# Attention's rows, their low halves and a router step in another order on VectorE, in a fused attention and expert kernel

## The chip, the cores and the metric

One core of a Trainium2 chip. The metric is the device time of one launch in microseconds; the time of a kernel is the median of its runs. The core has five engines that run their own instruction queues in order: TensorE (PE: matrix products; weight loads stand as PEld), VectorE (DVE), ScalarE (ACT), GpSimd (POOL) and SyncE (SP), which here only issues transfers. They wait for one another on semaphores.

## The reference

A pre-norm block of a sequence model, in float32, with x of 4 sequences of 2048 tokens of 256 numbers:

```python
x = x + attn(layernorm(x))     # causal linear attention, 16 heads of 16
#   q = elu(x Wq + bq) + 1, k = elu(x Wk + bk) + 1, v = x Wv + bv
#   s += k v^T ; z += k ; row = (q s) / (q z + 1e-6) ; out = rows Wo + bo
x = x + moe(layernorm(x))      # 8 experts 256 -> 512 (gelu) -> 256
#   each token goes to its top 2 experts by logits, weighted by a softmax of the two
```

## The kernel before

The program has two parts. The first, on which the change bears, is a chain of iterations over the sequence; the second runs the experts on tiles of 256 token rows and is untouched.

Attention works in steps of 128 tokens of each of the 4 sequences (`b` = 0 to 3), 16 steps in all. Each tile that feeds a product is split into a high half and a low half in float16 (value minus high), so that products of float16 tiles keep nearly float32 accuracy: ScalarE writes the high half, VectorE (for q and k: GpSimd) the low one. The names end in `_hi`/`_high` and `_lo`/`low`.

The iterations are pipelined over four stages, and the function `body(j, c)` of each engine writes its part of iteration `c` by hand, in the order in which the engine's queue will run it:

- `fr`, the front of step c: norm 1 of x, transposes (`x_transposes`), projections of q and k (`project(0)` to `project(3)`, `feature`, `qk_high`), values of v, and the transfers that stack the parts of q and k.
- `bk`, attention of step c - 1: for each b four groups of scores, `scores(b, n)` on TensorE, `score_hi(b, n)` on ScalarE, `score_lo(b, n)` on VectorE; then `attend(b)` (48 small products with the values, and the update of the state), `attention(b)` on VectorE (division by the denominator, L1293 to L1300, tile `at`), `state_part(b)` (L1309), the transpose of the rows (`out_transpose`, L693, into pA), their halves (`out_hi` L1031, `out_lo` L1314, tile `aT`), `out_project(b)`, and `residual(b)`, which adds x, writes `x1` (L1340) and takes the statistics of norm 2. Row 3 of a step is finished in the next iteration.
- `ro`, the router of step c - 2: norm 2 (`norm2_shift` L1287, `norm2_apply` L1039), and `router()` on VectorE: logits (L1367, L1369), top 2 of 8 (L1373, L1377), counts (L1386).
- `sc`, step c - 3: TensorE sums the counts (`route_positions`), VectorE makes the slots (`router_slots`), GpSimd scatters the rows to the experts' lists in memory.

Iterations 0 and 1 fill the pipeline; 2 to 15 have a front, 16 to 18 drain it. `STEPS` is 16. During the iterations the weights of the experts are loaded and split as well (`w1_high` on ScalarE, `w1_low` L1415 on VectorE), and `norm1_stats`, `norm1_shift` (L1254) prepare x of the next step.

All of TensorE's projection results go through a few banks of PSUM. Bank pA is shared by the transposed rows, the router's logits and the output projection, so the transposes of row b wait for the logits of the row before (`lga_done`), and `out_project(b)` waits until `residual` of the row before has read the bank (`x1_done`).

In VectorE's order around the change, of which iteration 6 is looked at below, the pieces stand so: xT's low halves (L1274), score_lo(0, 0), out_lo(3), residual(2), score_lo(0, 1), row data, score_lo(0, 2), residual(3), score_lo(0, 3), slots, score_lo(1, 0), norm2_shift, attention(0), state_part(0), score_lo(1, 1), statistics of x, out_lo(0), score_lo(1, 2), and so on, and at the end out_lo(2), router, attention(3), state_part(3), the logits of row 2.

Of the kernel before, what the change touches and what calls it, by code (L numbers as in the profile page):

```python
# [104 lines left out]
def build(nc, x, wqkvo, bqk, bv, bo, rw, w1, b1, w2, b2, cf, ch, cb, cm, out):  # L105
# [5 lines left out]
    with ExitStack() as ctx:  # L111
# [443 lines left out]
        def _(pe):  # L555
# [9 lines left out]
            def body(j, c, front=True, back=True):  # L565
# [120 lines left out]
                def out_transpose(s, b):  # L686
                    g = 4 * s + b
                    pe.wait_ge(at_done, g + 1)
                    if g:

                        pe.wait_ge(lga_done, g)
                    for k in range(KC):
                        mm = nc.tensor.transpose(pA[:, k * C:(k + 1) * C], at[:, k * P:(k + 1) * P], ident)  # L693
                    mm.then_inc(aT_ps, 1)
# [234 lines left out]
        def _(act):  # L929
# [27 lines left out]
            def body(j, c, front=True, back=True):  # L957
# [143 lines left out]
                if fr:  # L1101
                    feature_exp(2)
                    qk_high(1)
                normed = ro and c != STEPS + 1
                if bk:
                    out_hi(s, 0)
                    score_hi(1, 2)
                    score_hi(1, 3)
                if fr:
                    feature(3)  # L1110
                    qk_high(2)
                if normed:
                    norm2_apply(0)
                if bk:
                    score_hi(2, 0)
# [8 lines left out]
                if normed:  # L1124
                    norm2_apply(1)
                if bk:
                    out_hi(s, 1)
                    score_hi(2, 2)
                if normed:
                    norm2_apply(2)  # L1130
# [92 lines left out]
        def _(dve):  # L1223
# [33 lines left out]
            def body(j, c, front=True, back=True):  # L1257
# [102 lines left out]
                def router():  # L1360
# [3 lines left out]
                    if c >= 4:  # L1364
# [5 lines left out]
                                                   ALU.mult, ALU.mult))  # L1370
                    carry_wait(dve)
# [120 lines left out]
                if sc and c not in (STEPS, STEPS + 1):  # L1492
                    router_slots()
                if bk:
# [10 lines left out]
                elif ro and c != STEPS + 1:  # L1505
                    norm2_shift()
# [7 lines left out]
                if bk:  # L1514
                    score_lo(1, 1)
                if ahead:
                    norm1_stats(i + 1, 0, 2)
                if c == STEPS + 1:
                    router()
                    for b in range(B):  # L1520
                        norm2_apply(b)
                if bk:
                    out_lo(s, 0)
# [11 lines left out]
                if bk:  # L1535
                    score_lo(2, 0)
                    residual(s, 0)
                    attention(1)
# [3 lines left out]
                    score_lo(2, 2)  # L1542
                if ahead:
# [3 lines left out]
                if bk:  # L1547
                    score_lo(2, 3)
# [16 lines left out]
                if ro and c != STEPS + 1:  # L1565
                    router()
                if bk:
                    attention(3)
                    state_part(3)
                    logit_part(s, 2)  # L1570
                if c == 1 and not front:
# [377 lines left out]
```

## Time and profile before

| | |
|---|---|
| median of 3 runs | 1016.1 us (1013.57 to 1018.55) |
| profiled execution, its time / its span | 1024.98 us / 1023.2 us |
| TensorE, weight loads busy | 913.0 us (89%), 740.2 us (72%) |
| VectorE, ScalarE, GpSimd busy | 758.2 us (74%), 680.7 us (67%), 658.2 us (64%) |
| iterations | to about 580 us, experts from about 603 us |
| granted TensorE clock, mean | 0.974 of full |

The span runs from the first to the last instruction of the profiled execution; the rest of its time lies around it. A busy share says how much of the span an engine had an instruction running. An engine that waits in its queue holds all that stands behind it, so the timelines are read for the idle time in front of an instruction, which stands in brackets with the engine and line that ended it.

### The profile page before, as it was taken

How to read it: one execution, taken by the hardware profiler on the slowest of the kernel's cores; microseconds unless marked ns; L12 is line 12 of the kernel's file. 1: busy time of each engine (PE TensorE's matmuls, PEld its weight loads, DVE VectorE, ACT ScalarE, POOL GpSimd, SP SyncE). 2: the span in 40 equal slices, each digit the busy share in tenths (PEclk: the TensorE clock that was granted, in tenths of full speed). 3: DMA queues.
4: the chain of work that ended last, by engine and by line, in shares of the span. 5: the costliest groups of instructions: out<-in, count | busy, mean ns of one | idle time of the engine just before them, and what ended most of it. 6: DMA issues, size and time to landing. Idle time of an engine off the chain costs nothing. (4 is left out here: it accounts for less than half of the span.)

```text
span 1023.2 us, 33647 instructions
## 1 busy us (share of the span) xinstructions
PE 913.0 (89%) x10722; PEld 740.2 (72%) x10723; DVE 758.2 (74%) x2280; ACT 680.7 (67%) x1295; POOL 658.2 (64%) x580
## 2 busy tenths in 40 slices
PE   6788899899989998999987559899999999999994
PEld 3577677767766677766766338678999999999994
DVE  5788788888898888889887566456666666666673
ACT  7868888898888888898875414445555555555552
POOL 3245877788778877887773543347655665656565
PEclk9999899999999999999998779999999999999998
DMA  6726744554455354645451743435655556555554
GB/s 172 203 76 204 249 126 147 170 161 136 150 152 176 124 152 149 182 128 147 139 156 44 283 136 69 69 60 94 95 95 90 98 89 98 89 98 88 94 92 50
DMA packets 102583, 131.31 MB, mean 128 GB/s; under 512 B 15056, under 2 KB 89296, under 8 KB 101648
## 3 DMA queue, kind: packets, MB, share of 16 engines
q1 hardware_dynamic: 74336, 92.54, 32.4%
q0 software_dynamic: 25680, 35.01, 18.6%
q10 hardware_dynamic: 2464, 2.38, 0.7%
q8 instruction: 64, 1.05, 0.5%
q14 instruction: 39, 0.32, 0.1%
HBM read 64.29 MB, written 65.60 MB: 127 GB/s over the span
## 5 line engine op out<-in xcount | busy, mean ns | idle before, releaser
L1907 POOL DMA_INDIRECT out<-yt,to_token x135 | 216.6, 1604 | 176.2 <-DMA out<-yt,to_token 80.4
L1269 DVE SCALAR_TENSOR_TENSOR ahl<-pS,ahl 128x512 f16<-128x512 f32 x240 | 161.2, 682 | 42.1 <-ACT ahl L980 39.7
L980 ACT ACTIVATE ahl<-pS 128x512 f16<-128x512 f32 x240 | 142.2, 599 | 49.8 <-PE pS L652 36.0
L1783 POOL DMA_INDIRECT expert_in<-xn,cur x128 | 131.1, 1024 | 30.8 <-issue 26.0
L1191 ACT ACTIVATE g<-pS,b1s 128x256 f32<-128x256 f32 (+1 forms) x140 | 57.3, 462 | 94.1 <-PE pS L562 94.1
L562 PE MATMUL pS<-gT,w1s 128*128 128x256 f16 (+1 forms) x840 | 96.8, 271 | 4.0 <-DVE gT L1697 4.0
L562 PE MATMUL pF<-w2s,ghl 128*128 x816 | 95.3, 273 | 2.4 <-issue 1.6
L1704 DVE TENSOR_TENSOR ghl<-g,ghl 128x1024 f16<-128x1024 f32 (+1 forms) x68 | 83.0, 1221 | 18.8 <-ACT ghl L1216 12.5
L1777 POOL TENSOR_TENSOR state<-state,ut 128x272 f32<-128x272 f32 x64 | 49.9, 779 | 72.2 <-DVE ut L1309 71.3
L562 PE MATMUL pU<-w2s,ghl 128*128 x804 | 94.4, 273 | 1.6 <-issue 1.1
L562 PE MATMUL pF<-xT,was 128*128 128x512 f16 x384 | 92.8, 379 | 3.2 <-DVE xT L1274 3.0
L673 PE MATMUL pO<-vhl,ahl 128*128 128x17 f16 x3072 | 90.4, 171 | 5.6 <-DVE ahl L1269 3.6
L673 PEld LDWEIGHTS pO<-vhl,ahl 128*128 128x128 f16 x3072 | 88.4, 96 | 8.5 <-DVE ahl L1269 4.4
L652 PE MATMUL pS<-qst,kst 128*128 128x256 f16 x480 | 92.9, 276 | 0.0
L562 PEld LDWEIGHTS pS<-gT,w1s 128*128 x840 | 80.6, 99 | 15.5 <-issue 5.2
L648 PE MATMUL pS<-cbs 128*128 128x384 bf16 x240 | 79.7, 332 | 12.7 <-DVE ahl L1269 9.1
L562 PEld LDWEIGHTS pF<-w2s,ghl 128*128 128x128 f16 x816 | 79.4, 98 | 13.0 <-issue 3.4
L562 PEld LDWEIGHTS pU<-w2s,ghl 128*128 128x128 f16 x804 | 78.1, 98 | 12.6 <-issue 3.1
L1191 ACT ACTIVATE g<-pO,b1s 128x256 f32<-128x256 f32 (+1 forms) x72 | 29.1, 459 | 77.6 <-PE pO L562 73.5
L1216 ACT ACTIVATE ghl<-g 128x1024 f16<-128x1024 f32 (+1 forms) x68 | 72.0, 1060 | 0.1
L652 PEld LDWEIGHTS pS<-qst,kst 128*128 128x128 f16 x480 | 47.5, 99 | 20.9 <-issue 1.1
L562 PEld LDWEIGHTS pF<-xT,was 128*128 128x128 f16 x384 | 36.1, 97 | 36.3 <-DVE xT L1274 3.7
(223 smaller groups left out, 2184.3 us busy)
## 6 DMA issues: line engine op xcount, KB each, us to landing
xg<-expert_in SPq DMA_DIRECT2D x64, 260.0 KB
qk_parts<-qkhl SPq DMA_DIRECT2D x64, 256.0 KB, 2.4
qst<-qk_parts SPq DMA_DIRECT2D x192, 64.0 KB
kst<-qk_parts SPq DMA_DIRECT2D x96, 128.0 KB
xs<-x SPq DMA_DIRECT2D x16, 512.0 KB
out<-x SPq DMA_DIRECT2D x16, 512.0 KB
w1raw<-w SPq DMA_DIRECT2D x16, 256.0 KB
w2raw<-w SPq DMA_DIRECT2D x4, 1024.0 KB, 7.0
```

The costliest lines, as they stand in the source:

```text
L562: mm = nc.tensor.matmul(out, lhs(a, k), rhs(b_, k), start=(t == 0), stop=(t == len(terms) - 1))
L648: nc.tensor.matmul(o[:].rearrange("p (h q) -> p h q", q=C)[:, :, 0:STACK], ident16, mask_first, start=True, stop=False, skip_group_check=True)
L652: mm = nc.tensor.matmul(o[:, e * 2 * C:(e + 1) * 2 * C], kst[:, sp_, pr, b * C:(b + 1) * C], qst[:, sp_, :, pr, b * C:(b + 1) * C], start= ...
L673: mm = nc.tensor.matmul(pO[:, h * VC:(h + 1) * VC], ahl[:, b % 2, a, h * C:(h + 1) * C], vhl[:, sp_, b_, b, h * VC:(h + 1) * VC], start=False,
L980: nc.scalar.activation(ahl[:, b % 2, 0, n * 4 * C:(n + 1) * 4 * C], score_bank(fr, n)[:], ACT.Relu).then_inc(sc_hi, 1)
L1191: nc.scalar.activation(g[:, p1, f, h * P:h * P + width], hidden[p1][f // 2][:, c0:c0 + width], ACT.Gelu, bias=b1s[:, bass.ds(e * FC + f, 1 ...
L1216: nc.scalar.activation(ghl[:, p1, 0, :, 0:n], g[:, p1, :, 0:n], ACT.Copy).then_inc(g_hi, 1)
L1269: V.scalar_tensor_tensor(ahl[:, b % 2, 1, cols], score_bank(fr, n)[:], 0.0, ahl[:, b % 2, 0, cols], ALU.max, ALU.subtract).then_inc(sc_lo, 1)
L1704: V.tensor_tensor(ghl[:, p1, 1, :, 0:n], g[:, p1, :, 0:n], ghl[:, p1, 0, :, 0:n], ALU.subtract).then_inc(g_lo, 1)
L1777: G.tensor_tensor(sb_, sb_, ut[:, b % 2], ALU.add).then_inc(state_new, 1)
L1783: G.indirect_dma_start(xg_dram, bass.IndirectOffsetOnAxis(ap=cur[:, qp, 2 * b + t:2 * b + t + 1], axis=0), xn2[:, qp, b], None).then_inc(s ...
L1907: G.indirect_dma_start(out, bass.IndirectOffsetOnAxis(ap=to_token[:, c % 2, s:s + 1], axis=0), yt[:, c % 2, s], None, compute_op=ALU.add). ...
```

## The change

VectorE's order is changed in five places, ScalarE's in four, and TensorE gets one wait:

- VectorE: `norm2_shift` goes in front of `score_lo(1, 0)`; `out_lo(s, 0)` in front of the first statistics of x; `attention(1)` in front of `residual(s, 0)`; `score_lo(2, 3)` in front of `norm1_shift` and `w1_low`; and `router()` is cut in two: the logits stay (`router_logits()`), the rest goes behind `attention(3)`, `state_part(3)` and the logits of row 2.
- ScalarE: `out_hi(s, 0)` goes in front of `qk_high(1)`; `score_hi(2, 0)` in front of `qk_high(2)` and `norm2_apply(0)`; `out_hi(s, 1)` and `score_hi(2, 2)` in front of `norm2_apply(1)`.
- TensorE: the transpose of row 1 also waits for `x1` of row 0, since `residual(s, 0)` now stands behind `attention(1)`.

No instruction is added or left out besides that wait, in iteration 17 the two pieces of the router follow each other as before.

```diff
--- before.py
+++ after.py
@@ -689,6 +689,8 @@
                     if g:
 
                         pe.wait_ge(lga_done, g)
+                        if b == 1:
+                            pe.wait_ge(x1_done, g)
                     for k in range(KC):
                         mm = nc.tensor.transpose(pA[:, k * C:(k + 1) * C], at[:, k * P:(k + 1) * P], ident)
                     mm.then_inc(aT_ps, 1)
@@ -1100,19 +1102,22 @@
                     score_hi(1, 1)
                 if fr:
                     feature_exp(2)
+                if bk:
+                    out_hi(s, 0)
+                if fr:
                     qk_high(1)
                 normed = ro and c != STEPS + 1
                 if bk:
-                    out_hi(s, 0)
                     score_hi(1, 2)
                     score_hi(1, 3)
                 if fr:
                     feature(3)
+                if bk:
+                    score_hi(2, 0)
+                if fr:
                     qk_high(2)
                 if normed:
                     norm2_apply(0)
-                if bk:
-                    score_hi(2, 0)
                 if c == 0:
                     normalise(1, 0)
                 if fr:
@@ -1121,11 +1126,11 @@
                     score_hi(2, 1)
                 if fr and c >= 2:
                     w1_high()
+                if bk:
+                    out_hi(s, 1)
+                    score_hi(2, 2)
                 if normed:
                     norm2_apply(1)
-                if bk:
-                    out_hi(s, 1)
-                    score_hi(2, 2)
                 if normed:
                     norm2_apply(2)
                 if bk:
@@ -1357,7 +1362,7 @@
                     ins.then_inc(rt, 1)
                     dve.wait_ge(rt, RT * step + links[0])
 
-                def router():
+                def router_logits():
                     links[0] = 0
                     dve.wait_ge(lga_done, 4 * r + 4)
                     dve.wait_ge(ln2_rs, r + 1)
@@ -1368,6 +1373,8 @@
                     dve.wait_ge(lg_sum, r + 1)
                     link(r, V.scalar_tensor_tensor(lg[:], lga[:, rp], 1.0 / WS, rs2[:].unsqueeze(2).to_broadcast([P, B, E]),
                                                    ALU.mult, ALU.mult))
+
+                def router():
                     carry_wait(dve)
                     for b in range(B):
                         ins = V.max(mx[:, b], lg[:, b])
@@ -1491,6 +1498,8 @@
                     V.tensor_scalar(ready[:, 0:1], base[0:1, 0:1], float(PRE * MT), -128.0, ALU.is_ge, ALU.mult).then_inc(ready_set, 1)
                 if sc and c not in (STEPS, STEPS + 1):
                     router_slots()
+                if ro and c not in (STEPS, STEPS + 1):
+                    norm2_shift()
                 if bk:
                     score_lo(1, 0)
                 if c == 1 and not front:
@@ -1502,8 +1511,6 @@
                     V.scalar_tensor_tensor(worh[:, 1], o, WS, worh[:, 0], ALU.mult, ALU.subtract).then_inc(wor_done, 1)
                 if c == STEPS:
                     row_data()
-                elif ro and c != STEPS + 1:
-                    norm2_shift()
                 if bk:
                     attention(0)
                     state_part(0)
@@ -1513,14 +1520,15 @@
                 ahead = nx or c == 1 and not front
                 if bk:
                     score_lo(1, 1)
+                    out_lo(s, 0)
                 if ahead:
                     norm1_stats(i + 1, 0, 2)
                 if c == STEPS + 1:
+                    router_logits()
                     router()
                     for b in range(B):
                         norm2_apply(b)
                 if bk:
-                    out_lo(s, 0)
                     score_lo(1, 2)
                 if ahead:
                     norm1_stats(i + 1, 2, 3)
@@ -1534,18 +1542,17 @@
                     norm2_shift()
                 if bk:
                     score_lo(2, 0)
+                    attention(1)
                     residual(s, 0)
-                    attention(1)
                     state_part(1)
                     score_lo(2, 1)
                     out_lo(s, 1)
                     score_lo(2, 2)
+                    score_lo(2, 3)
                 if ahead:
                     norm1_shift(i + 1)
                 if fr and c >= 2:
                     w1_low()
-                if bk:
-                    score_lo(2, 3)
                 if fr:
                     values(0)
                 if bk:
@@ -1563,11 +1570,13 @@
                 if c == STEPS + 1:
                     w2_low(0)
                 if ro and c != STEPS + 1:
-                    router()
+                    router_logits()
                 if bk:
                     attention(3)
                     state_part(3)
                     logit_part(s, 2)
+                if ro and c != STEPS + 1:
+                    router()
                 if c == 1 and not front:
                     w1_low()
 
```

## Rows read from the trace of the kernel before

**Rows 1.** Busy us by engine in two stretches; then clock, DMA share, GB/s.

```profile
102.10:135.50 33.40, 30.45 (x430) 23.77 (x429) 26.83 (x89) 26.66 (x51) 24.29 (x24) 0.90 0.76 229
202.14:235.57 33.43, 30.36 (x442) 23.55 (x441) 29.11 (x99) 28.29 (x54) 27.27 (x25) 1.00 0.50 152
```

**Rows 2.** TensorE, iteration 6: start us, us, operation, count, [idle before, releaser].

```profile
199.84 1.28 PE L673 MATMUL pO<-vhl,ahl 128*128 128x17 f16 x45
...
204.28 0.41 PE L693 MATMUL pA<-cfs,at 128*128 128x128 f32 x2 [0.72 <-DVE lga L1328]
...
205.56 1.46 PE L562 MATMUL pF<-xT,was 128*128 128x512 f16 x6
...
215.95 0.44 PE L693 MATMUL pA<-cfs,at 128*128 128x128 f32 x2 [0.25 <-DVE at L1300]
...
217.88 0.30 PE L562 MATMUL pA<-worh,aT 128*128 128x8 f16 x6 [0.43 <-DVE aT L1314]
...
227.87 0.34 PE L648 MATMUL pS<-cbs 128*128 128x384 bf16 x1 [0.72 <-DVE ahl L1269]
```

**Rows 3.** VectorE in order of time, same columns, same iteration.

```profile
200.94 0.37 DVE L1373 MAX8 mx<-lg 128x8 f32<-128x8 f32 x4
...
202.80 0.16 DVE L1293 TENSOR_SCALAR rden<-pO 128x16 f32<-128x16 f32 x1
...
204.05 1.28 DVE L1274 TENSOR_TENSOR xT<-pF,xT 128x512 f16<-128x512 f32 x2
...
213.40 0.69 DVE L1269 SCALAR_TENSOR_TENSOR ahl<-pS,ahl 128x512 f16<-128x512 f32 x1 [0.70 <-ACT ahl L980]
214.01 1.06 DVE L1287 SCALAR_TENSOR_TENSOR sh<-mv,rs 128x4 f32<-128x4 f32 x1
...
217.42 0.41 DVE L1314 TENSOR_TENSOR aT<-pA,aT 128x256 f16<-128x256 f32 x1
...
221.38 0.69 DVE L1269 SCALAR_TENSOR_TENSOR ahl<-pS,ahl 128x512 f16<-128x512 f32 x1 [0.98 <-ACT ahl L980]
...
226.47 0.74 DVE L1415 SCALAR_TENSOR_TENSOR w1s<-w1raw,w1s 128x512 f16<-128x512 f32 x1
```

**Rows 4.** ScalarE in order of time, same iteration.

```profile
216.43 0.43 ACT L1031 ACTIVATE aT<-pA 128x256 f16<-128x256 f32 x1
...
219.74 0.64 ACT L1013 ACTIVATE qkhl<-kf 128x512 f16<-128x512 f32 x1
...
220.75 0.60 ACT L980 ACTIVATE ahl<-pS 128x512 f16<-128x512 f32 x1
...
225.65 0.58 ACT L980 ACTIVATE ahl<-pS 128x512 f16<-128x512 f32 x1
```

**Rows 5.** GpSimd in order of time, same iteration.

```profile
213.89 1.16 POOL L1770 TENSOR_TENSOR qkhl<-qf,qkhl 128x512 f16<-128x512 f32 x1 [0.21 <-ACT qkhl L1013]
...
220.57 1.28 POOL L1766 TENSOR_TENSOR kf<-et,lt 128x512 f32<-128x512 f32 x1
```

**Rows 6.** All executions of line 1287: duration ns min/median/max, first and last start.

```profile
L1287 DVE SCALAR_TENSOR_TENSOR sh<-mv,rs x15: 164/1059/1127, 78.4 to 550.8; 128x4 f32<-128x4 f32 x15
```

**Rows 7.** All executions of line 1415, same columns.

```profile
L1415 DVE SCALAR_TENSOR_TENSOR w1s<-w1raw,w1s x16: 682/734/1570, 43.5 to 526.6; 128x512 f16<-128x512 f32 x16
```

**Rows 8.** VectorE in iteration 3: the wait for the next rows of x.

```profile
115.79 0.75 DVE L1247 BATCH_NORM_STATS2 st<-xs 128x6 f32<-128x256 f32 x2 [1.64 <-DMA xs<-x]
```

**Rows 9.** TensorE in iteration 3, behind that wait.

```profile
116.93 0.32 PE L562 MATMUL pA<-worh,aT 128*128 128x8 f16 x6 [2.16 <-DVE aT L1314]
117.11 1.44 PE L562 MATMUL pA<-was,aT 128*128 128x256 f16 x6
```

**Rows 10.** TensorE at the start of iterations 16 and 17.

```profile
538.33 0.41 PE L693 MATMUL pA<-cfs,at 128*128 128x128 f32 x2 [1.70 <-DVE lga L1328]
...
574.10 0.66 PE L693 MATMUL pA<-cfs,at 128*128 128x128 f32 x2 [1.25 <-DVE lga L1328]
```

**Rows 11.** VectorE at the end of iteration 16.

```profile
572.61 0.17 DVE L1293 TENSOR_SCALAR rden<-pO 128x16 f32<-128x16 f32 x1 [5.55 <-remote]
```

More of the change, by code:

```diff
@@ L1123, in body @@
                     w1_high()
-                if normed:
-                    norm2_apply(1)
                 if bk:
@@ L1128, in body @@
                     score_hi(2, 2)
+                if normed:
+                    norm2_apply(1)
                 if normed:
```

## Prediction, made before the changed kernel ran

> **What bounds the kernel now.** I read the page's table of slices first. The attention iterations fill the first 570 of 1023 us and the experts the rest. The change touches only the iterations, so I went there by windows. Iterations 4 to 15 are alike: twelve of them from 135.3 to 536.1 us, 33.4 us each. In iteration 6 no engine is full: TensorE is busy 30.36 of 33.43 us, VectorE 29.11, ScalarE 28.29, GpSimd 27.27 [rows 1]. Three in-order queues hand one another small tiles, and each waits a little for the others. So the views that decide are the timelines with their idle times. TensorE waits 0.72, 0.25, 0.43 and 0.72 us for VectorE, among shorter ones [rows 2]. VectorE waits 0.70 and 0.98 us for ScalarE, and spends 1.06 us on a four-column operation at line 1287 [rows 3]. That operation takes 0.16 at best and 1.06 in the median [rows 6]. It ends at 215.07, and GpSimd's low half, started at 213.89, ends at 215.05 [rows 3, 5]. I read it as VectorE held until GpSimd lets go.
>
> What follows is one walk through iteration 6 in the new order. Durations are those of the rows; I take 0.06 us from one engine's end to another's start. Times are on the old clock, so minus means earlier.
>
> **Start: the router behind attention(3).** Before, the router's tail stands in front of attention(3): 202.80 - 200.94 = 1.86 us from its first maximum on [rows 3]. Attention(3) could start as soon as TensorE's last attention products end, 199.84 + 1.28 = 201.12 [rows 2]; so it starts at 201.2. Attention, state and logits take 204.05 - 202.80 = 1.25, then the tail 1.86: xT's low half starts at 204.34, 0.29 later than 204.05, because VectorE now idles about 0.3 for those products. TensorE's transpose of row 3 no longer waits (0.72 gone). But project(0) must wait for the first of xT's two low halves (1.28 for both [rows 3]): 204.34 + 0.64 + 0.06 = 205.04 instead of 205.56 [rows 2]; then out_project(3) waits for the residual, and I get 0.29 to 0.34 earlier for TensorE and ScalarE, not 0.72. The position products of the router need its counts at 204.5, which is just before TensorE arrives there.
>
> **norm2_shift in front of score_lo(1, 0).** It meets the GpSimd operation ahead of that low half, feature(1), of the kind that takes 1.28 [rows 5] and that now runs from 212.0 to 213.3. Line 1287 has no work of its own beyond 0.16 [rows 6]. So it is held again, to about 213.3, but now mostly inside the 0.70 in which VectorE idled. score_lo(1, 0) starts at 213.2 (-0.2), and attention(0) right behind it at 213.8 instead of 214.99 (-1.19). If nothing held it, attention(0) would be at 213.6; if it were held for its full 1.06 from 212.35 it would be 213.9. TensorE's transpose of row 0 then goes at 215.26 instead of 215.95 [rows 2], without its wait.
>
> **Row 0 turned out first.** ScalarE's out_hi(0) goes from 216.43 [rows 4] to 215.74, right behind the transpose (0.44 long [rows 2]); qk_high(1) slips behind it, and the low half of q that GpSimd makes of it still comes before its turn. On VectorE out_lo(0) stands ahead of two statistics: 216.18 instead of 217.42 [rows 3] (-1.24), with an idle of 0.38 in front, since VectorE is there before ScalarE is done. TensorE's out_project(0) follows at 216.65 instead of 217.88.
>
> **score_hi(2, 0) in front of qk_high(2) and norm2_apply(0).** These two take 220.75 - 219.74 = 1.01 [rows 4], and the queue is 0.17 early, so score_hi(2, 0) goes from 220.75 to 219.57 (-1.18) and VectorE's row at 221.38 [rows 3] to 220.2, which leaves 0.34 of the 0.98 wait. The queue does not end earlier: qk_high(3) still waits for GpSimd's feature(3), 220.57 + 1.28 before, 0.34 earlier now [rows 5].
>
> **attention(1) in front of residual(0).** Row 1's attention starts near 220.8, behind score_lo(2, 0) (0.6 from start to start), 2 us earlier than when residual(0) (0.87) stood between and the wait of 0.98 before; its transpose at 222.4 (-1.4). Its 0.82 to the finished rows, the residual's 0.87 and the state's 0.35 bring VectorE to 222.85. The added wait for x1 on TensorE has nothing to wait for: the residual is done at 222.1. Behind it are the scores (2, 2) and all that follows on TensorE. With score_lo(2, 1) at 222.85 (-1.17) the scores (2, 3) go 1.16 earlier.
>
> **score_lo(2, 3) in front of norm1_shift and w1_low.** ScalarE's score_hi(2, 3) goes from 225.65 [rows 4] to 224.93, as out_hi(1) and score_hi(2, 2) pass norm2_apply(1). VectorE waits for it until 225.55, an idle of 0.85, then does norm1_shift and w1_low (0.74): w1_low starts at 226.3 instead of 226.47 [rows 3], values(0) at 226.96, 0.78 earlier. The 0.72 wait of TensorE at 227.87 [rows 2] goes. From there VectorE's old sequence of 6.5 us runs without idle to the end of the router's logits, 233.5. Then comes attention(3), which waits for the last products again (0.2): it starts near 233.7, and xT's low half of iteration 7 at 233.7 + 1.25 + 1.86 = 236.81. Minus 204.34 that is 32.47 us, 0.96 less than 33.43.
>
> Nothing here moves a transfer: SyncE sends the parts of q and k behind GpSimd's low halves, which come 0.34 earlier in the same order, and GpSimd's own scatters keep their places. Bounds of the 0.96. Above: if every handover is a tenth better, 1.1. Below: if ScalarE's and GpSimd's queues set the pace, the only gain is their 0.34.
>
> **The other iterations.** Twelve at 0.96: 11.5 us. Iterations 1 and 2 gain about 0.9 together (they have no router in front). Iteration 3 is longer by 2.5 us: VectorE waits 1.64 for x behind other transfers [rows 8], out_project(0) is queued behind that and starts 2.16 late, and then one product group takes 1.44 at a granted clock of 0.90 over the iteration [rows 1, 9]; the same group takes 0.81 elsewhere. Now out_lo(0) does not stand behind this wait. I count 1.0 for it, with 3.0 as its bound if the clock stays up. Iteration 16 has a wait of 1.70 for the logits [rows 10], of which the router's tail gives back about 1.2. At its end the sign turns: VectorE stands 5.55 us until 572.61 [rows 11], and before, the router lay in front of this gap. Now its 1.86 us can lie behind, and route_positions and the transpose at 574.10 wait for it [rows 10]: a loss of 2.0, or 0.4 if VectorE is released with TensorE's products instead. I take 2.0.
>
> Sum: 11.5 + 0.9 + 1.0 + 1.2 - 2.0 = 12.6 us less. The profiled execution took 1024.98 (span 1023.2) and would take 1012.4. The median of the runs is 8.9 lower, 1016.1; the same difference gives 1003.5.
>
> **The rivals.**
> ScalarE and GpSimd pace it. For it: ScalarE is busy 28.29 and GpSimd 27.27 us of an iteration [rows 1], and qk_high(3) waits for GpSimd's feature(3). Against: VectorE's share is higher. 12 x 0.34 + 0.9 + 1.0 + 1.2 - 2.0 = 5.2 less: 1010.9. Chance 0.15.
>
> w1_low collides with GpSimd. It reads two tiles of SBUF, as line 1287 does, and took up to 1.57 instead of 0.74 once [rows 7]; GpSimd's state addition is what runs next to it. In the walk it is done at 227.0, and the state addition starts at 227.2. If score_hi(2, 3) comes late, both meet and 0.83 of the 0.96 is lost in each iteration: 12 x 0.13 + 1.1 = 2.7 less, 1013.4. Chance 0.10. The Trainium skill (SBUF — State Buffer, Who interferes with whom) says that VectorE with two SBUF inputs and GpSimd exclude each other for a whole instruction, in order of issue; by it w1_low would lose the whole addition or nothing. Line 1287's end with GpSimd's agrees; for w1_low the rows give only the 0.83 of the longest execution.
>
> Slower: attention(3) waits. VectorE now does nothing between the router's logits and TensorE's last products, and the tail follows in full before xT's low half. This alone costs 0.29 each iteration, as worked out above; it decides once the second half of the iteration saves less than 0.29, for instance when out_lo(0), ahead of two statistics, idles more than its 0.38. Twelve at 0.29 and the 2.0 at the end: 5.5 more, 1021.6. Chance 0.07.
>
> No change: the early rows only wait elsewhere, as all engines have slack of 3 to 6 us. 1016, chance 0.06.
>
> **How the numbers follow.** Forecast 0.62: 1003.5, own range 998 to 1009. The low end is 12 x 1.1 + 0.9 + 3.0 + 1.2 - 0.4 = 17.9 less, 998.2. Eight in ten reaches up to 1012.5, over the first rival. Within 0.5% (about what a measurement of this kernel can tell) is 1011.0 to 1021.2. Faster: 0.62, most of the first rival and a little of the second, 0.74. Same: 0.18. Slower: 0.08.
>
> **What would show it.** Iterations of 32.5 us. TensorE's 0.72 at the transpose of row 3 gone, VectorE idle some 0.2 to 0.3 in front of attention(3) and 0.3 to 0.9 in front of out_lo(0) and score_lo(2, 3). Line 1287 near 0.9 us still. Iteration 3 without its low clock. The transpose at the end 2 us later relative to the end of iteration 16. Wrong would be: iterations of 33.1 or more, w1_low near 1.5 us, or VectorE's idle before attention(3) over 0.6.

## The result and the profile after

The changed kernel takes 1006.77 us in the median of four runs (1003.27 to 1007.93), the kernel before, run beside it, 1017.33. The ratio is 0.9892, 95% interval 0.9848 to 0.9935: 1.1% faster. The prediction said 1003.5 (1.2% less), own range 998 to 1009, and eight in ten up to 1012.5. The profiled execution took 1003.27, with a span of 1001.5.

The page's busy times, and the windows of iteration 3 and iteration 6 (columns as in [rows 1]):

```profile
PE 912.3 (91%) x10722; PEld 736.9 (74%) x10723; DVE 753.8 (75%) x2280; ACT 674.0 (67%) x1295; POOL 654.3 (65%) x580
```

```profile
97.22:132.65 35.43, 31.31 (x442) 24.39 (x441) 28.86 (x100) 28.07 (x54) 26.68 (x25) 0.95 0.82 245
199.71:232.19 32.48, 30.43 (x444) 23.40 (x442) 28.90 (x99) 27.73 (x56) 27.18 (x24) 1.00 0.52 156
```

Iteration 6 is 32.48 us long instead of 33.43 [rows 1], with the same work in it: TensorE is now busy 94% of it.

TensorE in that iteration, in the columns of [rows 2]:

```profile
198.76 0.38 PE L695 MATMUL pA<-cfs,at 128*128 128x128 f32 x2
...
200.45 1.47 PE L562 MATMUL pF<-xT,was 128*128 128x512 f16 x6 [0.24 <-DVE xT L1279]
...
210.71 0.38 PE L695 MATMUL pA<-cfs,at 128*128 128x128 f32 x2
...
212.02 0.30 PE L562 MATMUL pA<-worh,aT 128*128 128x8 f16 x6
...
218.93 0.34 PE L648 MATMUL pS<-cbs 128*128 128x384 bf16 x1 [0.68 <-DVE ahl L1274]
...
224.63 0.34 PE L648 MATMUL pS<-cbs 128*128 128x384 bf16 x1 [0.37 <-DVE ahl L1274]
```

The waits of 0.72 at the transposes of row 3, 0.25 at those of row 0 and 0.43 at out_project(0) [rows 2] are gone. Near the end of the iteration 0.37 is left of the 0.72, and project(0) has a new wait of 0.24 for xT's low half. The largest wait, 0.68 at 218.93, is new too: TensorE is now there before score_lo(2, 1), which as before stands behind attention(1), residual(0) and state_part(1). In sum TensorE's idle time fell from 3.07 us (33.43 - 30.36) to 2.05 (32.48 - 30.43).

VectorE, in the columns of [rows 3]:

```profile
196.60 0.17 DVE L1298 TENSOR_SCALAR rden<-pO 128x16 f32<-128x16 f32 x1 [0.29 <-PE pO L673]
...
199.71 1.28 DVE L1279 TENSOR_TENSOR xT<-pF,xT 128x512 f16<-128x512 f32 x2
...
207.89 0.65 DVE L1292 SCALAR_TENSOR_TENSOR sh<-mv,rs 128x4 f32<-128x4 f32 x1
...
211.54 0.42 DVE L1319 TENSOR_TENSOR aT<-pA,aT 128x256 f16<-128x256 f32 x1 [0.20 <-ACT aT L1033]
...
220.92 0.69 DVE L1274 SCALAR_TENSOR_TENSOR ahl<-pS,ahl 128x512 f16<-128x512 f32 x1 [0.77 <-ACT ahl L982]
221.53 0.15 DVE L1259 SCALAR_TENSOR_TENSOR sh<-mv,rs 128x4 f32<-128x4 f32 x1
221.60 0.23 DVE L1260 TENSOR_TENSOR sd<-ve,rs 128x4 f32<-128x4 f32 x1
221.75 0.68 DVE L1422 SCALAR_TENSOR_TENSOR w1s<-w1raw,w1s 128x512 f16<-128x512 f32 x1
```

The places are the forecast ones: 0.29 idle ahead of attention(3), 0.20 ahead of out_lo(0), 0.77 ahead of score_lo(2, 3), and norm2_shift (now L1292) still held. It ends with GpSimd's feature(1):

```profile
207.25 1.27 POOL L1775 TENSOR_TENSOR qf<-et,lt 128x512 f32<-128x512 f32 x1
```

The clearest row is the one of all transposes of attention's rows (TensorE, all 128 of them): who they waited for, in us and times. Before:

```profile
  DVE at L1300: 58.1, 77
  DVE lga L1328: 12.6, 15
```

and after:

```profile
  DVE at L1305: 5.3, 9
  DVE x L1345: 1.6, 2
```

Of those 58 us, 43.0 (47 times) were idle time of the weight loads, which run beside other products; so the sum is no gain in time, but it shows that the rows no longer come late. The 1.6 us ended by `x` (L1345) are the added wait: 0.85 in iteration 1 and 0.76 in iteration 16.

### The profile page after: what moved, and what is told of

It reads as the page before. It is cut to its first block and busy times, and to the rows that moved or that the text cites. A ratio compares the mean times of both kernels' runs of the same rounds, so it can differ in the third digit from the quotient of the medians.

```text
span 1001.5 us, 33662 instructions
## 1 busy us (share of the span) xinstructions
PE 912.3 (91%) x10722; PEld 736.9 (74%) x10723; DVE 753.8 (75%) x2280; ACT 674.0 (67%) x1295; POOL 654.3 (65%) x580
## 3 DMA queue, kind: packets, MB, share of 16 engines
q1 hardware_dynamic: 74336, 92.54, 33.1%
## 5 line engine op out<-in xcount | busy, mean ns | idle before, releaser
L673 PE MATMUL pO<-vhl,ahl 128*128 128x17 f16 x3072 | 87.5, 171 | 2.8 <-DVE ahl L1274 2.8
L673 PEld LDWEIGHTS pO<-vhl,ahl 128*128 128x128 f16 x3072 | 84.6, 96 | 6.0 <-DVE ahl L1274 3.8
```

What stands on the lines that cost most here:

```text
L673: mm = nc.tensor.matmul(pO[:, h * VC:(h + 1) * VC], ahl[:, b % 2, a, h * C:(h + 1) * C], vhl[:, sp_, b_, b, h * VC:(h + 1) * VC], start=False,
```

## Where the time went, stage by stage

The kernel before ran again beside several of the experiments (run e8 below, 1018.3 us, span 1016.5), 6.7 us shorter than its first profile. Both stand beside the changed kernel's profile here. Starts of TensorE's x transposes give the lengths; the experts' first product is the first transpose of their rows (L885 before, L887 after):

| us | before, first profile | before again | after | forecast |
|---|---|---|---|---|
| start to iteration 1 | 27.1 | 27.4 | 25.8 | no change |
| iterations 1 and 2 | 72.2 | 71.6 | 71.4 | -0.9 |
| iteration 3 | 35.9 | 33.5 | 35.4 | -1.0 |
| iterations 4 to 14, each | 33.42 | 33.41 | 32.53 | 32.47 |
| iteration 15 to the last transposes of rows | 71.2 | 64.0 | 61.0 | -0.2 |
| from there to the experts' first product | 28.9 | 32.4 | 32.4 | |
| experts | 420.2 | 420.2 | 417.7 | no change |

Over all runs here the experts' stretch lies between 416 and 422 us without an edit in it, the start before iteration 1 between 25.8 and 28.3, iteration 1 between 39.3 and 40.1, and iteration 3 between 33.5 and 37.8 while the padding rows are written in one burst. That is the noise against which a single profile is read; the mean period of iterations 4 to 14 repeats to 0.02.

## The experiments

Each run is one profiled execution beside one of the kernel before, except where a ratio is given.

### The router behind attention(3), alone, and left out

The kernel before, with only this edit:

```diff
-                if ro and c != STEPS + 1:
-                    router()
+                if ro and c != STEPS + 1:
+                    router_logits()
                 if bk:
                     attention(3)
                     state_part(3)
                     logit_part(s, 2)
+                if ro and c != STEPS + 1:
+                    router()
```

> The kernel before, with the router cut in two and its tail behind attention(3), nothing else moved. Three-queue theory (the walk of the prediction): the wait of 0.7 us for the logits at row 3's transpose goes, VectorE idles 0.1 to 0.3 us in front of attention(3), iterations of 33.0 us (0.4 less). Rival (the router's tail in front of xT only costs): 33.4 to 33.7 us. Rival (ScalarE and GpSimd pace, any part brings their 0.34): 33.1.

Measured: 1018.34 us beside 1018.51; iterations 4 to 14 take 33.17 instead of 33.41, iteration 3 takes 36.2. The edit by itself is worth 0.24 an iteration, close to the 0.29 that the walk gave TensorE at the iteration's start.

The opposite, the changed kernel with the router whole in front of attention(3):

> The changed kernel with the whole router in front of attention(3) again. Three-queue theory: TensorE waits again for the logits at row 3's transpose (about 0.8 us), iterations of 33.0 us instead of 32.5. Rival (the router's place doesn't matter once the rest is moved): 32.5. Rival (nearly all of the gain is the router's): 33.4.

Measured: 1008.99 us; iterations of 32.80. So the router's place is worth 0.27 with the other edits, and the other edits 0.61 without it. The two add up to the whole 0.88: hardly any interaction. The slower rival, attention(3) waiting at a cost of 0.29 each, is refuted: the wait of 0.29 is there (196.60 above), and the edit that makes it gains.

### score_lo(2, 3) behind norm1_shift and w1_low again

```diff
                     score_lo(2, 2)
-                    score_lo(2, 3)
                 if ahead:
                     norm1_shift(i + 1)
                 if fr and c >= 2:
                     w1_low()
+                if bk:
+                    score_lo(2, 3)
```

> The changed kernel with score_lo(2, 3) behind norm1_shift and w1_low again. Three-queue theory: VectorE's values(0) comes 0.55 us later, as norm1_shift waits for GpSimd, and nothing behind it has slack: iterations of 33.0 us. Rival (ScalarE and GpSimd pace the iteration): 32.5 to 32.6, the loss is taken up by TensorE's slack.

Measured: 1017.11 us. This single piece decides over the whole gain: of the eleven iterations 4 to 14, six take 33.07 to 33.43 and five (6, 8, 9, 11 and 13) 34.45 to 34.99; the mean is 33.86, longer than before the change. TensorE in one of the long ones:

```profile
225.49 0.34 PE L648 MATMUL pS<-cbs 128*128 128x384 bf16 x1 [1.60 <-DVE ahl L1274]
...
228.24 0.53 PE L648 MATMUL pS<-cbs 128*128 128x384 bf16 x1
228.55 0.64 PE L652 MATMUL pS<-qst,kst 128*128 128x256 f16 x2
```

and the granted clock behind that wait and at the same place of the next, short iteration, where TensorE waits just as long (1.59 at 259.95):

```profile
225.00:235.00 10.00, 9.51 (x157) 8.48 (x158) 8.38 (x27) 5.13 (x10) 4.40 (x6) 0.83 0.57 174
259.50:267.50 8.00, 7.55 (x151) 7.06 (x152) 7.45 (x22) 5.02 (x9) 3.78 (x6) 1.00 0.71 217
```

The edits ahead of this one bring TensorE to the scores (3, 1) sooner; with the low half of (2, 3) late, what they save becomes one wait of 1.6 us. Both kinds of iteration have it. In the short ones the products behind it keep 0.33 and 0.38 us, and the iteration loses 33.07 - 32.53 = 0.54. In the long ones they take 0.53 and 0.64 for a while, at a granted clock of 0.83 over 10 us (a mix of 2.4 and 1.2 GHz), and the iteration loses 1.6 more. So of the 1.33 that this piece is worth in the mean, 0.54 is the wait and nearly all the rest the clock. Why the same wait lowers it in five iterations and not in six is open.

### norm2_shift that GpSimd can't hold

```diff
-                    V.scalar_tensor_tensor(sh2[:], mv2[:, :, 0], -1.0, rs2[:], ALU.mult, ALU.mult).then_inc(ln2_sh, 1)
+                    for b in range(B):
+                        ins = V.tensor_scalar(sh2[:, b:b + 1], mv2[:, b, 0:1], rs2[:, b:b + 1], -1.0, ALU.mult, ALU.mult)
+                    ins.then_inc(ln2_sh, 1)
```

> The changed kernel, with norm2_shift as four VectorE instructions with one tile each from SBUF as input (mean times the factor, a number per partition, times -1) instead of one with two. If the second input is what holds the instruction while GpSimd works: none of them over 0.2 us, done before GpSimd's feature addition ends, and the iteration still 32.5 us, since score_lo(1, 0) then waits for ScalarE. If it is held for another reason (GpSimd busy at all, a late semaphore): the last of them ends with GpSimd's operation, about 0.6 us after the start.

Measured: 1007.47 us, iterations of 32.44. All executions of the line in this form (columns as in [rows 6]):

```profile
L1293 DVE TENSOR_SCALAR sh<-mv,rs x60: 202/205/215, 75.3 to 537.9; 128x1 f32<-128x1 f32 x60
```

The same values, the same GpSimd operation next to it, and 202 to 215 ns in all 60, against 164 to 1279 for the two-input form in the changed kernel:

```profile
L1292 DVE SCALAR_TENSOR_TENSOR sh<-mv,rs x15: 164/651/1279, 75.0 to 535.7; 128x4 f32<-128x4 f32 x15
```

In iteration 6 the four run from 210.71 to 211.29 beside GpSimd's feature(1), 210.07 to 211.33, and are not held. So the hold is shown, and so is that it costs nothing here: the four take 0.58 together where the held one took 0.65, and iterations 4 to 7, 9 and 10 take 32.41 to 32.49 in both kernels. The edit changes the operation's form and width along with the number of inputs; that it is the second input that is held fits, but was not taken apart. The mean period is 0.09 shorter than the changed kernel's 32.53, nearly all of it in iterations 11 to 14 (32.44 each instead of 32.53 to 32.77): there the changed kernel's VectorE stands 0.24 us (at 393.06) and 0.29 us (at 426.40) ahead of router instructions, ended by nothing that the profile names, and in this run it doesn't. That is not the hold. The prediction put 0.9 for the held operation; counted from xT's low half, norm2_shift starts 0.17 later than in the walk and feature(1) ends 0.15 earlier, which leaves 0.65.

### w1_low in the gap ahead of score_lo(2, 3)

```diff
                     score_lo(2, 2)
-                    score_lo(2, 3)
-                if ahead:
-                    norm1_shift(i + 1)
                 if fr and c >= 2:
                     w1_low()
+                if bk:
+                    score_lo(2, 3)
                 if fr:
                     values(0)
+                if ahead:
+                    norm1_shift(i + 1)
```

> The changed kernel, with VectorE's order score_lo(2, 2), w1_low, score_lo(2, 3), values(0), norm1_shift: w1_low (0.60 us from start to start), which needs nothing of GpSimd, fills the 0.77 us in which VectorE waits for score_hi(2, 3). Three-queue theory with VectorE's queue as the pace behind score_lo(2, 3): values(0) 0.82 us earlier, norm1_shift 0.22 behind it, iterations of 31.9 us instead of 32.45. Rival (ScalarE and GpSimd pace that half): 32.4, and VectorE's idle only moves to its next wait.

Measured: 1003.63 us, beside 1016.03; iterations of 32.56, no gain. VectorE, and GpSimd beside it:

```profile
220.80 0.68 DVE L1422 SCALAR_TENSOR_TENSOR w1s<-w1raw,w1s 128x512 f16<-128x512 f32 x1
221.66 0.69 DVE L1274 SCALAR_TENSOR_TENSOR ahl<-pS,ahl 128x512 f16<-128x512 f32 x1 [0.17 <-ACT ahl L982]
222.26 0.68 DVE L1352 SCALAR_TENSOR_TENSOR v<-pF,bvs 128x512 f32<-128x512 f32 x1
222.86 0.15 DVE L1259 SCALAR_TENSOR_TENSOR sh<-mv,rs 128x4 f32<-128x4 f32 x1
222.93 0.78 DVE L1260 TENSOR_TENSOR sd<-ve,rs 128x4 f32<-128x4 f32 x1
```

```profile
222.59 1.04 POOL L1793 DMA_INDIRECT expert_in<-xn,cur  x1 [0.20 <-issue]
```

The gap is filled: 0.17 idle is left of the 0.77. But the four columns of norm1_shift's second operation, 0.155 in the median before and in the changed kernel (0.23 in its iteration 6), now take 0.78 and end within 0.1 us of GpSimd's scatter (222.59 + 1.04 = 223.63). Its median over the run is 782 ns. The operation just ahead of it (222.86), beside the same scatter and with two inputs too, takes its plain 0.15. What was saved is handed back at once.

That reading names a repair, and the repair tests it: the same, with the multiply that was held put in front of attention(3), where VectorE idles 0.29.

```diff
-                V.tensor_tensor(sd1[:, i % 2], ve1[:], rs1[:], ALU.mult).then_inc(sd1_done, 1)
+                if first or now:
+                    norm1_scale(i)
+
+            def norm1_scale(i):
+                V.tensor_tensor(sd1[:, i % 2], ve1[:], rs1[:], ALU.mult).then_inc(sd1_done, 1)
...
                 if ro and c != STEPS + 1:
                     router_logits()
+                if ahead:
+                    norm1_scale(i + 1)
                 if bk:
                     attention(3)
```

> The run with w1_low in the gap, and line 1255 (the scale of x's logits, two tiles from SBUF, held for 0.78 us beside GpSimd's scatter there) moved to stand in front of attention(3), where VectorE waits 0.29 us for TensorE anyway. If that held instruction is what ate the 0.6 us: nothing on VectorE between values(0) and residual(1) but 0.1 us, iterations of 31.9 to 32.0 us. Rival (ScalarE and GpSimd pace the second half, the held instruction was harmless): 32.45.

Measured: 995.87 us beside 1020.63; iterations of 31.79, 0.77 less than with w1_low's move alone. The multiply takes 164 ns in the median. Moving 0.155 us of work brought 0.77, so 0.6 of it was the hold.

### The padding rows, two transfers an iteration

```diff
-                if c == 2:
-
-                    sp.wait_ge(pads_set, 4)
-                    for n in range(E):
+                if 2 <= c < 2 + E:
+
+                    if c == 2:
+                        sp.wait_ge(pads_set, 4)
+                    for n in (c - 2,):
...
-                if c == 3:
+                if c == 3 + E:
```

> The changed kernel, with the sixteen transfers of padding rows that SyncE issues behind iteration 2 spread over iterations 2 to 9, two in each. If the extra 3 us of iteration 3 are the wait for x behind these transfers: iteration 3 takes 32.5 to 33 us instead of 35.4, and the others stay at 32.45. If it is another thing of that iteration (the first scatters, code): 35 us as before.

Measured: 1003.6 us; iteration 3 takes 32.52, like any other. In the changed kernel it took 35.43. There VectorE waits for x, and TensorE behind VectorE:

```profile
111.26 0.42 DVE L1319 TENSOR_TENSOR aT<-pA,aT 128x256 f16<-128x256 f32 x1 [0.20 <-ACT aT L1033]
114.09 0.75 DVE L1252 BATCH_NORM_STATS2 st<-xs 128x6 f32<-128x256 f32 x2 [2.41 <-DMA xs<-x]
```

```profile
115.50 0.37 PE L648 MATMUL pS<-cbs 128*128 128x384 bf16 x1 [2.77 <-DVE ahl L1274]
115.67 0.63 PE L652 MATMUL pS<-qst,kst 128*128 128x256 f16 x2
```

SyncE's queue shows why x is late: sixteen transfers of padding stand ahead of it, and it is issued at 107.28.

```profile
93.59 0.43 SPq L500 DMA_DIRECT2D expert_in<-pads  x1
...
105.70 0.72 SPq L502 DMA_DIRECT2D out<-pads  x1
...
107.28 0.74 SPq L425 DMA_DIRECT2D xs<-x  x1
```

x's arrival sets this iteration, not VectorE's order. out_lo(0) did get in front of the wait, as forecast, but the low clock stayed: 0.95 over the iteration, products of 0.38 taking 0.63. The wait for x is 2.41 us instead of 1.64 [rows 8]; over all profiles with the burst it lies between 0.24 (the kernel before, again) and 3.90 (w1_low in the gap), so that difference says nothing of the order.

### The last router in front again

The changed kernel, with `router()` ahead of attention(3) in iteration 16 alone.

> The changed kernel, with the router's tail in front of attention(3) in iteration 16 alone, where the prediction booked a loss of 2.0 us. If that loss is real: the transpose of row 3 in iteration 17 and the table of tiles come 1.5 to 2 us earlier relative to the start of iteration 16. If not: the same within the scatter of this stretch, or 0.4.

Measured: 1007.65 us. The end of this one, TensorE first, then GpSimd and VectorE:

```profile
548.88 1.38 PE L673 MATMUL pO<-vhl,ahl 128*128 128x17 f16 x48 [0.64 <-DVE ahl L1274]
...
552.96 0.66 PE L695 MATMUL pA<-cfs,at 128*128 128x128 f32 x2 [0.98 <-DVE lga L1333]
```

```profile
564.73 0.96 POOL L1794 DMA_INDIRECT expert_in<-xn,cur  x1 [6.85 <-issue]
565.71 1.04 POOL L1760 TENSOR_TENSOR rs<-ve,cfs 128x4 f32<-128x4 f32 x1
```

and TensorE and VectorE of the changed kernel at the same place:

```profile
546.49 1.38 PE L673 MATMUL pO<-vhl,ahl 128*128 128x17 f16 x48 [0.64 <-DVE ahl L1274]
...
551.43 0.42 PE L695 MATMUL pA<-cfs,at 128*128 128x128 f32 x2
```

```profile
563.87 0.19 DVE L1372 TENSOR_TENSOR lga<-lga,bor 128x32 f32<-128x32 f32 x1 [6.43 <-POOL rs L1758]
```

From the last attention products to the transposes it is 552.96 - 548.88 = 4.08 with the router in front and 551.43 - 546.49 = 4.94 behind. The loss that the prediction booked is there, in its place, with 0.86 us instead of 2.0. But it does not reach the end: VectorE then stands for GpSimd's rs, 7.63 us here and 6.43 in the changed kernel, and GpSimd comes to it only after a stand of 6 to 7 us between two scatters, in both kernels. From iteration 15 to the experts' table of tiles it is 87.0 us in the changed kernel and 87.8 with the router in front; in the runs that leave this stretch alone it is 86.2 to 87.0. So the last router's place in front brings nothing to the end, by one profile of each.

### The kernel before, again

> The kernel before, unchanged, profiled a second time, to see which stretches of its first profile repeat. Iterations 4 to 15 should be 33.4 us again, iteration 3 35 to 36. Its first profile took 1024.98 us against a median near 1017; if the excess lies behind iteration 16 (engines standing while the second layer's weights load), that stretch is about 6 us shorter here.

Measured: 1018.3 us. Iterations 4 to 14 take 33.41, as in the first profile. Iteration 3 takes 33.48 (VectorE waits only 0.24 for x), and VectorE's 5.55 at the end [rows 11] is not there; GpSimd's stand is, with 6.21. So of the three single waits with which the prediction priced iterations 3 and 16, two ([rows 8, 11]) did not come again; the third, 1.70 at the start of iteration 16 [rows 10], is there again with 1.69.

### GpSimd's rstd ahead of the scatter

GpSimd, iteration 17: `rs` of norm 2 is computed before the 16 scatters and not between them.

```diff
-                if c == STEPS + 1:
-                    scatter(0)
                 if ro:
                     rstd(r, ve2, rs2, ln2_ve, ln2_rs)
+                if c == STEPS + 1:
+                    scatter(0)
```

> The changed kernel, with GpSimd's reciprocal root of the last norm 2 in front of the two scatters that stand before it in iteration 17. GpSimd stands about 6.3 us between those two scatters, and VectorE waits for the root behind them. If the stand belongs to the scatter (its queue): the router comes 4 to 5 us earlier and TensorE's table products too, the scatters last. If it comes at a time or place of its own whatever the instruction: the same stretch, within 1 us.

Measured: 1003.56 us, with an iteration 3 of 36.8. GpSimd:

```profile
560.29 1.04 POOL L1758 TENSOR_TENSOR rs<-ve,cfs 128x4 f32<-128x4 f32 x1 [3.14 <-DVE ve L1243]
...
564.69 0.96 POOL L1792 DMA_INDIRECT expert_in<-xn,cur  x1 [2.12 <-issue]
```

rs starts 6.0 us after the last transposes (554.25), where it was 11.3; the stand is 2.12 us instead of 6.27. From the last transposes to the experts' first product it is 29.0 us instead of 32.4. The stand ends 10.4 us after the last transposes here and 10.3 in the changed kernel: it belongs to a time and not to an instruction. Which time, the fourteen profiles taken together tell. SyncE begins to issue the experts' second weights, 1 MB a transfer, at 547.41 here and at 544.61 in the changed kernel, and in every profile the stand ends 16.4 to 17.7 us after that issue; counted from the last transposes it ends after anything from 6.3 to 11.8 us. So the stand goes with these loads; that they cause it was not tried.

### ScalarE's order as it was

The changed kernel with `out_hi(s, 0)`, `score_hi(2, 0)`, `out_hi(s, 1)` and `score_hi(2, 2)` in their old places on ScalarE; VectorE's five edits stay.

> The changed kernel with ScalarE's whole order as before; VectorE's new order and TensorE's wait stay. Three-queue theory: score_hi(2, 0) 1.0 us later, so attention(1) too, most of which VectorE's idle of 0.18 and 0.77 us behind takes up: iterations of 32.7 us (0.2 more). Rival (VectorE's early places are worth nothing without ScalarE's): 33.1, what the router alone gives.

Measured: 1005.61 us; iterations 4 to 14 of 32.53, the same to 0.01. VectorE in iteration 6 of this run:

```profile
212.87 0.42 DVE L1317 TENSOR_TENSOR aT<-pA,aT 128x256 f16<-128x256 f32 x1 [0.71 <-ACT aT L1033]
...
217.10 0.69 DVE L1272 SCALAR_TENSOR_TENSOR ahl<-pS,ahl 128x512 f16<-128x512 f32 x1 [0.58 <-ACT ahl L982]
...
221.74 0.69 DVE L1272 SCALAR_TENSOR_TENSOR ahl<-pS,ahl 128x512 f16<-128x512 f32 x1 [0.28 <-ACT ahl L982]
```

VectorE waits 0.71, 0.58 and 0.28 us for ScalarE where the changed kernel has 0.20, none and 0.77, and 0.18 at score_lo(2, 1): 0.4 more in sum, spread otherwise. From xT's low half score_lo(2, 3) starts 21.21 us later in both (220.92 - 199.71, 221.74 - 200.53). What ties ScalarE is its wait for GpSimd's last half of k, in the changed kernel

```profile
217.03 0.63 ACT L1015 ACTIVATE qkhl<-kf 128x512 f16<-128x512 f32 x1 [0.78 <-POOL kf L1775]
```

and it comes 17.32 us after xT in both (217.85 - 200.53 there). The pieces moved ahead of it were moved within time that ScalarE then waits out. In iterations 4 to 14 the four edits on ScalarE are worth nothing.

Iteration 16, which has no front, is another matter. TensorE at the transposes of row 1, this run and the changed kernel:

```profile
539.91 0.41 PE L695 MATMUL pA<-cfs,at 128*128 128x128 f32 x2 [1.47 <-DVE x L1343]
```

```profile
538.40 0.41 PE L695 MATMUL pA<-cfs,at 128*128 128x128 f32 x2 [0.76 <-DVE x L1345]
```

With ScalarE's old order this wait is 0.7 longer, and the products behind it run at half clock for about 3 us (0.63 where they take 0.38). From iteration 15 to the last transposes it is 62.4 us instead of 61.0, where the runs with ScalarE's new order and the router behind have 60.3 to 61.8. So these edits bring about 1.4 us once, at the end, on the word of one profile.

### The best of the runs put together

w1_low in the gap with the multiply ahead of attention(3), the one-input norm2_shift, the padding rows spread, rstd ahead of the scatter.

> The version put together from the runs: the changed kernel with w1_low in the gap ahead of score_lo(2, 3), norm1_shift behind values(0) and its multiply ahead of attention(3), norm2_shift as four one-input operations, the padding rows written one transfer an iteration, and GpSimd's rstd ahead of the scatter in iteration 17. If the gains are independent: iterations 4 to 14 of 31.7 to 31.8 us (31.79 with the multiply ahead of attention(3) alone; the one-input form alone brought 0.09, of which part may be the same idle time), iteration 3 of about 31.8 instead of 34.9 (-3.1), and from the last transpose to the experts' start 29.0 instead of 32.5 (-3.4). From the 995.87 of that one run this makes 989.4; with the scatter of the experts' stretch (416 to 422 us over the runs) 987 to 994, a ratio of 0.970 to 0.977 to the kernel before. Rival: the edits share one idle time, since each leaves TensorE nearer to its busy 30.4 of an iteration and ScalarE and GpSimd then set the pace: iteration 3 and the end gain, the period stays 31.8, and four one-input operations in place of a held one cost or gain nothing. A third: the early arrival at the end of the iterations only lengthens GpSimd's stand while the experts' weights load, and the experts' start comes 0 to 1 us earlier than without it: 993.

Measured, five runs: 987.97 us (987.2 to 991.79) beside 1018.55; ratio 0.9712, interval 0.9689 to 0.9735, 2.9% faster than the kernel before and 1.8% faster than the changed one by the two ratios. Its iteration 3 and an ordinary iteration:

```profile
96.48:128.30 31.82, 30.11 (x443) 23.39 (x442) 29.01 (x102) 27.65 (x54) 26.84 (x25) 1.00 0.55 173
191.80:223.54 31.74, 30.10 (x442) 23.39 (x441) 29.08 (x102) 27.65 (x54) 27.38 (x25) 1.00 0.61 185
```

Iterations of 31.76, iteration 3 without a low clock, 28.8 us from the last transposes to the experts. The one-input form brings nothing in an ordinary iteration (31.74 with and without it), and 0.04 in the mean. TensorE is busy 95% of the iteration.

## Why the prediction was right

The forecast was right for the reason given: VectorE's order hands TensorE its tiles sooner, 0.9 us in each of twelve iterations. That the sum of the other terms also came near is luck, as the last three points show. Point by point:

- **The period.** 32.47 was forecast, iteration 6 took 32.48 and the mean of iterations 4 to 14 is 32.53: 12 x 0.88 = 10.6 us instead of 11.5. Iterations 4 to 10 take 32.45 in the mean, 0.02 from the walk; the rest is lost in iterations 11 to 14, two of which have the unnamed stands of VectorE described above.
- **The router behind attention(3).** TensorE and ScalarE 0.29 to 0.34 earlier, project(0) then gated by xT's low half: the gate is there (0.24), the gain is 0.24 to 0.27 (first two runs).
- **norm2_shift.** Held again and harmless, as said; 0.65 instead of 0.9.
- **Row 0 first.** The transposes of row 0 and out_project(0) lost their waits. The idle time ahead of out_lo(0) is 0.20, not 0.38. The share given to ScalarE's side of it is refuted: with ScalarE's old order the period is the same.
- **score_hi(2, 0) and attention(1).** VectorE's wait of 0.98 [rows 3] is 0 in the changed kernel, not 0.34, and 0.18 appears at the next low half; the added wait for x1 costs nothing in an ordinary iteration (no idle time at the transposes of row 1 in iteration 6), but TensorE does stand on it in iterations 1 and 16, 0.85 and 0.76 us. And of the 1.18 that the walk passed on from ScalarE nothing was needed in the ordinary iterations.
- **score_lo(2, 3).** Idle 0.77 ahead of it (0.85 forecast), and w1_low unheld at 0.68. I had it as one step among six; it carries the result, since without it the others' gain turns into one wait and a lower clock. norm2_shift, out_lo(0) and attention(1) on VectorE were not undone by themselves, so how much of the 0.61 is each one's stays open.
- **Iterations 1 and 2.** 0.9 was booked; iteration 2 gains 0.7 against both profiles of before, and iteration 1 varies by 0.8 over the runs.
- **Iteration 3: mis-sized.** The step was that out_lo(0) no longer stands behind the wait for x, worth 1.0. x's arrival behind the padding rows sets this iteration, and it gained 0.5 against one profile of before and lost 1.9 against the other. The row [rows 8] was one draw of a wait that lies between 0.24 and 3.90 us.
- **Iteration 16: mis-sized.** Its start gave 1.3, against 1.2 booked. Its body, for which nothing was booked, gave 1.6 more (541.32 to 559.86 in the repeat of before, 529.52 to 546.49 after). Of that 1.1 is the wait at the transposes of row 1 (1.83 in the repeat, 0.76 after), and the rest are products that ran at half clock behind the longer wait. By the run with ScalarE's old order, 1.4 of the 1.6 are ScalarE's edits.
- **The end: mis-sized.** 2.0 was booked, the transposes are 0.86 later, and GpSimd's stand hides even that.

Forecast sum 12.6. Against the repeat of the kernel before the profile gives 15.0, of which 4.0 (start 1.5, experts 2.5) lie where nothing was changed. The medians give 10.6: the profiled execution of the changed kernel lies 3.5 below its median, that of the repeat 1.0 above. Outside iterations 4 to 15 the forecast had 1.1 in sum; against the repeat these stretches gave 0.20 in iterations 1 and 2, lost 1.95 in iteration 3 and gave 2.16 from iteration 16 to the last transposes, 0.4 together. Terms that were wrong by 1 to 3 us each cancelled.

Of the rivals, a pace set by ScalarE and GpSimd (periods of 33.1) is out. w1_low's collision did not come, although in the changed kernel it runs beside a scatter of GpSimd's (from 221.63, 1.04 long), as it did before; the like of it came one operation away, in norm1_shift, as soon as I moved w1_low myself.

The Trainium skill (SBUF — State Buffer, Who interferes with whom) says that a VectorE operation with two SBUF inputs contends with a GpSimd one that reads SBUF, and that one with a single input, outside VectorE's two-port modes, does not. The one-input run agrees with that (202 to 215 ns against up to 1279). The 0.78 beside a scatter looks like the same hold on one operation, while w1_low, also with two inputs from SBUF, took its plain 0.68 beside a scatter, and norm1_shift's first operation its plain 0.15; the runs do not settle what tells them apart.

## What to carry to other kernels

Where three in-order queues feed one another, walk one period through in the new order with the durations of the trace, and read the period alone; the single long waits of one profile (here 1.64 and 5.55 us) are charged only after a second profile shows them. Undo each piece of a reordering by itself: here one of the nine edits on VectorE and ScalarE decided between 1.1% faster and no gain, and four were worth nothing in the ordinary iterations because their queue waits for another engine right behind. A short operation that reads two tiles of SBUF next to GpSimd's can stand for several times its work: here 0.16 us stood for 0.65 to 0.78, which was free in front of an idle gap and cost 0.6 an iteration elsewhere.

## What the runs showed of the hardware

- A 128x4 operation of VectorE with two SBUF inputs takes 0.15 to 2.30 us by what GpSimd does at the time: beside a 128x512 operation it ends with it (at 208.54 and 208.52 in the changed kernel), beside a 128x1024 one too (from 17.31 to 19.61, GpSimd from 17.24 to 19.59), and beside a scatter one took 0.78 and another 0.15. The same work as four operations with one input takes 0.58 and never more.
- With score_lo(2, 3) back in its old place, the same wait of 1.6 us of TensorE, in iterations that are otherwise nearly full, is followed by products at half clock in five of eleven iterations (0.53 us for 0.33, 0.83 granted over 10 us) and by none in the other six, and costs 1.6 us more where it is. In iterations 4 to 14 of all other profiles no single wait of TensorE is over 1.00 us, and the granted clock is 1.00.
- In iteration 17 GpSimd stands 6.2 to 6.9 us between two scatters of 1 us in ten profiles (4.8 in the one-input run, 2.2 in the first profile of before), ended by nothing that the trace names; with rstd ahead of the scatter in its queue the stand was 2.1 and 2.0. In all fourteen profiles it ends 16.4 to 17.7 us after the first issue of the experts' second weights.
